# Graph attention, Trainium2: every second subtraction of the row maxima goes to TensorE as a fourth matmul pass

## What is computed

```
scores = jnp.einsum('ehd,ehd->eh', q[src], k[dst])
smax = jax.ops.segment_max(scores, src, num_segments=N)
ex = jnp.exp(scores - smax[src])
denom = jax.ops.segment_sum(ex, src, num_segments=N)
attn = ex / denom[src]
out = jax.ops.segment_sum(attn[:, :, None] * v[dst], src, num_segments=N)
```

## Time and profile before

| | |
|---|---|
| median of 3 runs | 3067.86 us (3063.8 to 3068.15) |
| profiled execution | 3068.89 us, its span 3067.1 us, so 1.8 us lie around the span |
| mean granted TensorE clock | 0.972 of full |
| TensorE matmul busy | 2871.9 us (94%), weight loads 1810.2 us (59%) |
| VectorE busy | 2059.3 us (67%) |
| ScalarE, GpSimd busy | 810.1 us (26%), 765.6 us (25%) |
| chain that ended last | TensorE 69%, VectorE 21%, issue 5% |
| attention steps, first to last subtraction | 462.7 to 2172.5 us, with the MLPs of blocks 0 to 2 in between |

### The profile page before, as it was taken

One profiled execution on the slowest core, in us unless ns is written; L12 is line 12 of the kernel. 1 busy time (PEld: TensorE's weight loads), 2 busy tenths in 40 slices (PEclk: granted clock), 3 DMA queues, 4 the chain that ended last, 5 costly groups with the idle time before them and its releaser, 6 DMA issues.

```text
span 3067.1 us, 31231 instructions
## 1 busy us (share of the span) xinstructions
PE 2871.9 (94%) x11230; PEld 1810.2 (59%) x11230; DVE 2059.3 (67%) x3698; ACT 810.1 (26%) x1152; POOL 765.6 (25%) x701
## 2 busy tenths in 40 slices
PE   5878899999999999999999999999999999999999
PEld 1245556676556666556667555667645566556555
DVE  9999856786757776756777765778787876623211
ACT  1154442223212222221222321222322213213221
POOL 5732403343023334022334130334410000000000
PEclk9989999999999999999999999999999999999999
DMA  3000110000300000310000220000245244421001
GB/s 83 17 8 1 42 55 1 1 28 30 125 21 14 1 28 14 117 45 14 1 28 1 86 90 14 1 28 1 69 124 153 66 130 141 127 82 38 14 0 34
DMA packets 74679, 143.61 MB, mean 47 GB/s; under 512 B 11429, under 2 KB 11820, under 8 KB 74525
## 3 DMA queue, kind: packets, MB, share of 16 engines
q1 hardware_dynamic: 68988, 129.58, 13.6%
q0 software_dynamic: 5536, 12.03, 1.2%
HBM read 130.66 MB, written 10.92 MB: 46 GB/s over the span
## 4 chain that ended last, share of the span: by engine, by line
PE 69%; DVE 21%; issue 5%; ACT 3%; DVEq 1%; DMA 1%; POOL 0%; POOLq 0%; SPq 0%
PE ps L1547 14%; PE ps L1777 11%; PE ps L1806 10%; PE ps L1658 6%; PE ps L1751 4%; PE ps L1538 4%; DVE prob L1025 4%; DVE x L1015 3%; PE ps L1500 2%; PE ps L1798 2%; PE ps L1564 2%; PE ps L1647 2%; PE ps L1632 2%; DVE ps L971 2%; DVE onehot_src L896 2%
## 5 line engine op out<-in xcount | busy, mean ns | idle before, releaser
L703 POOL TENSOR_TENSOR pacc<-pacc,prob 125x628 f32<-125x628 f32 (+1 forms) x288 | 405.3, 1407 | 348.9 <-DVE prob L1044 348.9
L1547 PE MATMUL ps<-yT,w 128*128 128x416 f32 (+1 forms) x1152 | 442.5, 541 | 18.5 <-DVE qk_lo L962 11.6
L1658 PE MATMUL ps<-prob,big 125*128 125x314 f32 x1280 | 393.8, 430 | 14.0 <-DVE prob L1044 10.7
L1366 ACT ACTIVATE prob<-prob 125x628 f32<-125x628 f32 x320 | 233.0, 728 | 572.8 <-DVE prob L1025 572.8
L1806 PE MATMUL ps<-pieces,counts_r 125*125 125x512 f32 x1400 | 355.8, 409 | 0.0
L1547 PEld LDWEIGHTS ps<-yT,w 128*128 128x128 f32 x1152 | 229.0, 201 | 206.8 <-issue 195.5
L1044 DVE SCALAR_TENSOR_TENSOR prob<-prob,typed 125x628 f32<-125x628 f32 x320 | 260.3, 813 | 70.4 <-ACT prob L1366 68.2
L1806 PEld LDWEIGHTS ps<-pieces,counts_r 125*125 125x125 f32 x1400 | 259.1, 187 | 77.6 <-issue 17.4
L1647 PE MATMUL ps<-qk_hi 128*125 128x314 f32 x640 | 270.1, 422 | 11.2 <-DVE prob L1025 10.6
L1658 PEld LDWEIGHTS ps<-prob,big 125*128 125x128 f32 x1280 | 227.6, 190 | 81.0 <-DVE prob L1044 27.2
L1025 DVE TENSOR_TENSOR prob<-ps,shift 125x628 f32<-125x628 f32 x320 | 257.3, 804 | 4.4 <-PE ps L1649 3.7
(11 more groups left out here) (213 smaller groups left out, 4411.2 us busy)
## 6 DMA issues: line engine op xcount, KB each, us to landing
basis<-in_basis SPq DMA_DIRECT2D x160, 256.0 KB, 2.7
lite_ring<-in_basis SPq DMA_DIRECT2D x120, 256.0 KB, 2.6
w<-in_m_w SPq DMA_DIRECT2D x8, 1024.0 KB, 6.7
w<-in_wk SPq DMA_DIRECT2D x5, 1024.0 KB, 6.7
w<-in_wv SPq DMA_DIRECT2D x4, 1024.0 KB, 5.6
w<-in_wq SPq DMA_DIRECT2D x4, 1024.0 KB, 5.4
oT<-in_cw SPq DMA_DIRECT2D x8, 512.0 KB, 3.8
w<-in_wo SPq DMA_DIRECT2D x4, 1024.0 KB, 5.4
```

Of the source, the lines that this page charges most:

```text
L703: nc.gpsimd.tensor_tensor(pacc[:, c0:c0 + nn], pacc[:, c0:c0 + nn], prob[:, n % 3, p0:p0 + nn], ALU.add).then_inc(psum_done, 1)
L1366: A.activation(prob[:, n % 3, :], prob[:, n % 3, :], ACT.Exp, scale=DH ** -0.5).then_inc(exp_done, 1)
L1547: last = mm(lin_ps(job, 128, nn), weight[:, k, m * 128:(m + 1) * 128], lhs[:, k, c0:c0 + nn], start=(k == 0), stop=(k == KD - 1))
L1658: last = mm(o_halves[:, b, :], vrow[:, t, h * DH:(h + 1) * DH], prob[:, n % 3, b * QUARTER:(b + 1) * QUARTER], start=(t == 0), stop=(t == ...
```

## The change

In steps for which `subtracted` is false, the subtraction on VectorE is left out. TensorE adds the maxima in the same accumulation: a fourth pass per quarter, with the 125 x 125 matrix `first_row` (first row ones, else zeros) as weights and the columns of `shift` as the moving operand, so that row 0 of `shift` is added to every row. ScalarE's exp reads the scores in PSUM itself, waits for `score_full` and for the `prob` buffer, and its `exp_done` frees the score slot. `subtracted` is false for the odd steps of head 0 and for the odd steps from 11 on of heads 1 and 2: 10 + 5 + 5 = 20 of a block's 80, 80 of 320. `shifted` is counted over the remaining ones. `shift` becomes F32R; two more clears on VectorE make `first_row`.

```diff
--- before.py
+++ after.py
@@ -179,6 +179,18 @@
 SCORES = {(s.kind, s.h, s.j): s for s in plan_scores()}
 SCORES_PER_BLOCK = len(SCORES)
 EXPS = MAXES = HEADS * 2 * T
+
+
+def subtracted(h, j):
+    return h == HEADS - 1 or (h > 0 and j < T) or j % 2 == 0
+
+
+SHIFT_NO = {}
+for _h in range(HEADS):
+    for _j in range(2 * T):
+        if subtracted(_h, _j):
+            SHIFT_NO[_h, _j] = len(SHIFT_NO) + 1
+SHIFTS = len(SHIFT_NO)
 
 
 def build(nc, a, out):
@@ -407,7 +419,8 @@
         junk = pacc[:].bitcast(F16)[:, 0:N]
         cw = sl("cw", [128, 4, D], F32R)
         stage = oT[:, 0:2 * D].rearrange("p (a d) -> p a d", d=D)
-        shift = sl("shift", [P, N], F32)
+        shift = sl("shift", [P, N], F32R)
+        first_row = sl("first_row", [P, P], F32R)
         bias_r = sl("bias_r", [P, D], F32R)
         two_rows = sl("two_rows", [P, P], F32R)
         bcol = sl("bcol", [128, 3, KD], F32)
@@ -878,8 +891,10 @@
             V.memset(condS[:, N:N + 2].bitcast(F32), 0.0)
             V.memset(two_rows[:].bitcast(F32), 0.0)
             V.memset(ident_r[:].bitcast(F32), 0.0)
+            V.memset(first_row[:].bitcast(F32), 0.0)
             V.drain()
             V.tensor_copy(ident_r[:, 0:P], ident[0:P, 0:P])
+            V.memset(first_row[0:1, :].bitcast(F32), 1.0)
             V.memset(two_rows[0:1, :].bitcast(F32), 1.0)
             V.memset(two_rows[32:33, :].bitcast(F32), 1.0)
             V.drain().then_inc(blk_done, 1)
@@ -1022,7 +1037,7 @@
                     if n >= 3:
                         dve.wait_ge(pv_done, at(i, EXPS, n - 2))
                         dve.wait_ge(psum_done, at(i, EXPS, n - 2))
-                    V.tensor_tensor(in_quarters(prob[:, n % 3, :]), score_ps(s.slot), in_quarters(shift[:, c0:c0 + HALF]),
+                    V.tensor_tensor(in_quarters(prob[:, n % 3, :]), score_ps(s.slot), in_quarters(shift[:, c0:c0 + HALF].bitcast(F32)),
                                     ALU.add).then_inc(shifted, 1)
 
                 if i == 0:
@@ -1037,7 +1052,8 @@
 
                         n = h * 2 * T + j
                         t, c0, nn = j % T, HALVES[j // T], HALF
-                        shift_scores(h, j)
+                        if subtracted(h, j):
+                            shift_scores(h, j)
                         if h + 1 < HEADS:
                             masked_max(h + 1, j)
                         dve.wait_ge(exp_done, at(i, EXPS, n + 1))
@@ -1362,8 +1378,17 @@
                 for h in range(HEADS):
                     for j in range(2 * T):
                         n = h * 2 * T + j
-                        act.wait_ge(shifted, at(i, EXPS, n + 1))
-                        A.activation(prob[:, n % 3, :], prob[:, n % 3, :], ACT.Exp, scale=DH ** -0.5).then_inc(exp_done, 1)
+                        if subtracted(h, j):
+                            act.wait_ge(shifted, at(i, SHIFTS, SHIFT_NO[h, j]))
+                            A.activation(prob[:, n % 3, :], prob[:, n % 3, :], ACT.Exp, scale=DH ** -0.5).then_inc(exp_done, 1)
+                        else:
+                            s = SCORES["exp", h, j]
+                            act.wait_ge(score_full, at(i, SCORES_PER_BLOCK, s.n + 1))
+                            if n >= 3:
+                                act.wait_ge(pv_done, at(i, EXPS, n - 2))
+                                act.wait_ge(psum_done, at(i, EXPS, n - 2))
+                            A.activation(in_quarters(prob[:, n % 3, :]), score_ps(s.slot), ACT.Exp,
+                                         scale=DH ** -0.5).then_inc(exp_done, 1)
                         if j == T:
                             copy_o(h, 0)
                     if h + 2 < HEADS:
@@ -1620,7 +1645,10 @@
                         if b.kind == "max":
                             pe.wait_ge(max_done, at(i, MAXES, b.h * 2 * T + b.j + 1))
                         else:
-                            pe.wait_ge(shifted, at(i, EXPS, b.h * 2 * T + b.j + 1))
+                            if subtracted(b.h, b.j):
+                                pe.wait_ge(shifted, at(i, SHIFTS, SHIFT_NO[b.h, b.j]))
+                            else:
+                                pe.wait_ge(exp_done, at(i, EXPS, b.h * 2 * T + b.j + 1))
 
                 def max_scores(h, j):
 
@@ -1646,7 +1674,9 @@
                         o = score_ps(s.slot)[:, b, :]
                         mm(o, hi[:, 1, rows], hi[:, 0, cols], start=True, stop=False)
                         mm(o, hi[:, 1, rows], lo[:, 0, cols], start=False, stop=False)
-                        last = mm(o, lo[:, 1, rows], hi[:, 0, cols], start=False, stop=True)
+                        last = mm(o, lo[:, 1, rows], hi[:, 0, cols], start=False, stop=subtracted(h, j))
+                        if not subtracted(h, j):
+                            last = mm(o, first_row[:], shift[:, cols], start=False, stop=True)
                     last.then_inc(score_full, 1)
 
                 def weighted_values(h, j):
```

## The result

The changed kernel takes **3084.56 us** (median of 6 runs, 3078.22 to 3091.89) against 3068.01 of the kernel before (6 runs, 3063.80 to 3068.66): ratio 1.006, 95% interval 1.0047 to 1.0073. It is slower by 16.5 us, or 0.6%, which is clear of the noise; 3083 with 3064 to 3103 was forecast. The profiled execution took 3083.14, its span is 3081.4.

What follows compares the result with a forecast made beforehand. TensorE (2.22 us a step) and the VectorE-ScalarE loop (2.33) were within 5%, TensorE binding after the change. Terms 0.17+0.63+0.36+2.88-0.43 = 3.61 a block, 14.4 in four, plus 0.3 for clears: +14.7, giving 3083; range 3064 to 3103.

Steps and rivals of the forecast that it cites:

- TensorE's floor of 2.22, odd steps 2.51, pair 4.73: Plain steps of heads 0 to 2: TensorE bounds both; even steps 2.22 us, odd 2.51, a pair 4.73 against 4.66.
- Rival A: Plain steps: TensorE has about 0.5 us room a step, only the score-slot loop binds; -16 us, 3053; chance 0.14.
- The fourth pass at 0.145 each: Changed steps: two added TensorE passes at 0.145 us each, 0.29 a step, 23 us in all.
- D: Changed steps: each added pass costs a full-precision pass; 160 x 0.12 = +19 us, 3103; chance 0.03.
- Hand-overs in time: Plain steps: the score slot is free before TensorE wants the next weights, 2.30 against 2.40 us in odd steps.
- B: Plain steps: new hand-overs late each time, weights of 29 steps a block stay exposed; +12 us, 3095; chance 0.10.
- Steps 11 and 12, +0.96 a head, 2.88 a block: Heads 0 to 2: step 11's exp stands behind ScalarE's output-half copy, TensorE waits nearly 1.6 us; +0.96 a head.
- E: Steps 11 and 12: the output-half copy costs what it did, only small terms stay; +3 us, 3072; chance 0.08.
- Steps 0 to 19 of heads 0 to 2: Per block: head 0 steps 2 to 10 +0.17, steps 13 to 18 +0.63, steps 11 and 12 in three heads +2.88.
- VectorE, about 58 us less busy: 80 subtractions removed, 0.73 us each as spacing: 58 us of VectorE work, nearly none of it TensorE's.
- End of head 2, -0.43: After step 19's mask product, which comes 2.53 us after the first pass instead of 2.96: -0.43 us a block.
- C: The 12 longer waits lower TensorE's clock, 3.4 us lost after each; +41 us, 3124; chance 0.05.

Runs made afterwards that it cites:

- three passes: Changed kernel with the third score pass left out in the 80 fourth-pass steps, so TensorE has six score passes: 3069.1 us, ratio 1.0006 to the kernel before.
- with and without step 11: With: kernel before plus the fourth pass in step 11 only of heads 0 to 2, 3079.4 us. Without: changed kernel, no fourth pass in step 11, 3082.5 us.
- The moved copy: Changed kernel with ScalarE's copy of the first output half after the exp of step 11 instead of before it: 3066.1 us.
- 8 repeated passes: Kernel before with the two maxima passes of step 19 of heads 0 and 1 issued five times over, 8 more passes: 3084.5 us.
- the 4: Kernel before with the two maxima passes of step 19 of heads 0 and 1 issued three times over, 4 more passes: 3085.2 us.
- head 3's fourth pass: Kernel before with the fourth pass only in odd steps from 11 on of head 3, copy of the first output half as before: 3050.6 us.

## Why the prediction was right

Step by step, against its own numbers:

- **TensorE's floor of 2.22, odd steps 2.51, pair 4.73.** Measured 2.22 and 2.52, pair 4.74. Rival A fell here, and more plainly with three passes, where an odd step at once became shorter by the passes taken out, but for the first half of head 0. The rule of the Trainium skill that A leaned on (Perfetto Trace Analysis, Identifying the Most-Contended Engine) would have called TensorE 79% loaded; in these steps the spacing of starts was the measure that held.
- **The fourth pass at 0.145 each.** Measured 0.15; D fell.
- **Hand-overs in time.** No load exposed in plain steps; B fell. Two details were off. Step 1 of head 0, taken as unchanged, took 2.22 instead of 2.33. And the load behind it does wait for the exp, 0.75 us, so there are 16 such waits and not the 12 forecast.
- **Steps 11 and 12, +0.96 a head, 2.88 a block.** Measured 4.15 + 2.22 = 6.37 against 5.45 before, +0.92; E fell. The kernels with and without step 11 show it from two sides (8.6 and 10.9 us). The moved copy shows it from a third: it takes away TensorE's whole wait, 1.6 us in each of 12 places and so 19.4 us, more than the change had added there.
- **Steps 0 to 19 of heads 0 to 2.** The forecast's terms for them are 0.17 + 0.63 + 2.88 = 3.68 a block, 14.7; measured 14.1.
- **VectorE, about 58 us less busy.** Measured 44.6. The forecast left the mask product at its length; it grew by 11 us (last section). This had no part in the time, since TensorE was the bound.
- **End of head 2, -0.43.** In block 2 it went from 9.59 to 9.12 us, -0.47; in the other three blocks a stretch at 0.50 falls there and hides the gain (9.68 to 10.07). The ends of heads 0 and 1 cost 0.28 instead of 0.18, read on those where the clock is the same.
- **The clock.** Here the forecast was right in total and thin in its reasons. C priced stretches at 0.50 after each long wait; there is none in the heads. But the clock did move elsewhere. At the start of head 3 the changed kernel runs slow in blocks 1 and 2, where the kernel before didn't, and for twice as long as it in blocks 3 and 4 (windows of the changed kernel: head 2 of block 2, then the start of head 3):
```profile
1102.90:1155.30 52.40, 50.48 (x251) 39.50 (x249) 47.63 (x81) 14.30 (x21) 25.10 (x18) 1.00 0.12 41
...
1164.40:1172.00 7.60, 7.34 (x29) 5.17 (x28) 4.23 (x8) 1.45 (x2) 1.75 (x2) 0.78 0.00 0
```
It won at the ends of head 0 in three blocks (-1.4 each) and lost there in block 2 (+1.9). The sum happened to be about +2 in the median. The other kernels show that it could as well have been more: against the kernel before, the clock takes 8 us more with the 8 repeated passes, 14 more with the 4, 15 more without step 11. So the agreement of 3083 with 3084.6 to 2 us is partly luck; that of 14.7 with 14.1, in the steps where the clock is the same, is not. A forecast for this kernel should have carried some 10 us for the clock from the start; the range did, for other reasons.

## What to carry to other kernels

When two engines are within 5% of each other, add up what each needs for one period without its stalls before moving work between them: a stall that is released by the other engine hides how full the first one is. Moving the release of a buffer to another in-order engine also moves it behind everything queued there; look for the one step where that engine waits for something else, and reorder that. And the same edit belongs where the receiving engine has room: at full clock 80 steps with the fourth pass in heads 0 to 2 lost some 15 us, 11 of them behind the copy, and 20 in head 3 won some 10.

## What was not expected of the hardware

- **The granted clock can outweigh the change that is being measured.** 4.5 us more work gave 17 us more time, with the same instructions at nearly the same places at 0.50 for longer. It goes the other way as well: head 3's fourth pass came with 6 us less taken. Across the kernels here what the clock takes lies between 80 and 101 us on average, so a comparison of two versions needs the time x clock beside the time, or the steps themselves.
- **VectorE's mask product gets longer beside GpSimd's sum.** It reads and writes SBUF alone, and takes 0.81 us in the earlier trace rows, where the sum of the step before is nearly over. In the changed kernel's odd steps it starts while the sum runs and takes 1.20 (952.02 to 953.22 above, the sum before it ending at 952.55). Of the 320 mask products 68 start with more than 0.2 us of the sum ahead, and every one of them ends 0.67 us after the sum's end; the other 252 keep their 0.81. The kernel before has none of the first kind. It cost nothing in the changed kernel, since VectorE had slack, but it ate 11 us (260.3 to 271.1) of the 64 that the subtractions gave back. With three passes, where VectorE is the bound of the first half of head 0, it takes 1.62 us and holds the subtraction up.
- **The exp reads PSUM faster than SBUF**: 0.693 us (80 of them) against 0.728.
